# A three-layer transformer block on one core: when the last stage's base product is made, and which engine empties the FFN's sum banks

## The reference

```python
x = x + xattn0(layernorm(x), ctx)        # 32 query heads on 8 kv heads, RMS norms, Wo
x = x + ffn0(layernorm(x))               # 4-bit weights; silu(x Wg) * (x Wu), times Wd; 512 -> 1376 -> 512
x = x + xattn1(ctx, layernorm(x), ctx)   # softmax over tokens of ctx^T x, times ctx; no weights
x = x + ffn1(layernorm(x))
# ffn1:
base   = einsum('bsi,oi->bso', x, W_org)
q      = einsum('bi,ki->bk', x.mean(axis=1), Wq)
coeffs = softmax(einsum('bk,ek->be', q, lora_keys) / sqrt(128))
h      = einsum('bsi,eir->bser', x, lora_down)
delta  = einsum('be,bser,ero->bso', coeffs, h, lora_up)
return base + delta
```

## Time and profile before

| | us |
|---|---|
| median of 3 runs (lowest, highest) | 1201.81 (1201.21, 1204.52) |
| the profiled execution, its time | 1201.67 |
| its span | 1199.9 |
| TensorE busy in it | 1127.4 (94%) |
| VectorE, ScalarE, GpSimd busy | 755.0, 542.7, 416.3 |

### The profile page before, as it was taken

How to read it: one execution, slowest core, us unless ns; L and a number is a source line. 1 busy time by engine, 2 the same in 40 slices (tenths; PEclk the granted TensorE clock), 3 DMA queues, 4 the chain that set the end, 5 groups by cost and what they waited for, 6 DMA issues and landing times. The chain is left out here.

```text
span 1199.9 us, 19956 instructions
## 1 busy us (share of the span) xinstructions
PE 1127.4 (94%) x6643; PEld 963.4 (80%) x6643; DVE 755.0 (63%) x1572; ACT 542.7 (45%) x1437; POOL 416.3 (35%) x421
## 2 busy tenths in 40 slices
PE   4899999999999999999999988789999999898998
PEld 3799899898899898899899878567777777676776
DVE  7555555555555555555555777799954666687863
ACT  4444554544454544454544544343323445454541
POOL 4433332332322332323332433154422324554531
PEclk7999999999999999999999999999999999798999
DMA  6211111101011101011100010022202245133300
GB/s 210 76 36 33 26 33 32 36 23 35 24 35 32 34 25 35 23 36 32 33 19 11 22 46 1 18 80 80 75 25 54 62 106 124 43 74 77 88 1 36
DMA packets 48731, 56.65 MB, mean 47 GB/s; under 512 B 10822, under 2 KB 29270, under 8 KB 48620
## 3 DMA queue, kind: packets, MB, share of 16 engines
q1 hardware_dynamic: 48620, 55.26, 17.2%
HBM read 40.56 MB, written 2.10 MB: 36 GB/s over the span
## 5 line engine op out<-in xcount | busy, mean ns | idle before, releaser
L387 PE MATMUL bank<-wqkv,kvT 128*128 128x256 f32 x1536 | 201.2, 288 | 8.7 <-DVE vv L577 8.6
L387 PEld LDWEIGHTS bank<-wqkv,kvT 128*128 128x128 f32 x1536 | 189.3, 193 | 10.6 <-DVE vv L577 10.6
L432 PE MATMUL bank<-wo,aoT 128*128 128x512 f32 x768 | 192.0, 399 | 5.7 <-DVE acc L573 5.7
L375 PE MATMUL bank<-wqkv,kvT 128*128 128x512 f32 x768 | 189.2, 396 | 5.6 <-issue 4.0
L375 PEld LDWEIGHTS bank<-wqkv,kvT 128*128 128x128 f32 x768 | 141.7, 191 | 33.2 <-issue 6.2
L432 PEld LDWEIGHTS bank<-wo,aoT 128*128 128x128 f32 x768 | 139.5, 188 | 33.3 <-DVE aoT L568 6.3
L673 POOL TENSOR_TENSOR rms<-msq,half_neg 128x4 f32<-128x4 f32 x64 | 64.4, 1007 | 226.0 <-DVE msq L584 225.8
L560 ACT ACTIVATE prob<-bank,nmax 128x128 f32<-128x128 f32 x256 | 90.3, 372 | 2.1 <-DVE nmax L597 2.1
L538 ACT ACTIVATE qsq<-bank 128x512 f32<-128x512 f32 x64 | 38.2, 597 | 117.0 <-PE bank L375 117.0
L1916 POOL TENSOR_TENSOR pr<-pr,rc 128x512 f32<-128x512 f32 x64 | 66.6, 1044 | 70.7 <-DVE rc L1785 70.6
L676 POOL TENSOR_TENSOR rms<-msq,half_neg 128x2 f32<-128x2 f32 x64 | 44.6, 696 | 134.1 <-DVE msq L593 134.1
(11 more groups left out here) (176 smaller groups left out, 2210.3 us busy)
## 6 DMA issues: line engine op xcount, KB each, us to landing
wqkv_raw<-in_L_xattn_Wq_dram SPq DMA_DIRECT2D x32, 256.0 KB, 2.5
wo_raw<-in_L_xattn_Wo_dram SPq DMA_DIRECT2D x32, 256.0 KB, 2.7
qS<-qhl SPq DMA_DIRECT2D x32, 256.0 KB, 3.8
kS<-chl SPq DMA_DIRECT2D x32, 128.0 KB, 3.0
packed<-_L_ffn_gate_qweight_dram SPq DMA_DIRECT2D x40, 64.0 KB, 2.3
packed<-in_L_ffn_up_qweight_dram SPq DMA_DIRECT2D x40, 64.0 KB, 2.3
packed<-_L_ffn_down_qweight_dram SPq DMA_DIRECT2D x10, 256.0 KB
acc<-in_x_dram SPq DMA_DIRECT2D x8, 256.0 KB, 5.6
```

Of the source, the lines that this page charges most:

```text
L375: mm = pe.matmul(b_q[:, :], kvT[:, l, kt, p, 1:3, :], wqkv[:, par, r, kt, 0:QW], start=(kt == 0 and n == 0), stop=(kt == KT - 1 and n == 2))
L387: mm = pe.matmul(b_kv[:, b * 256:(b + 1) * 256], kvT[:, l, kt, p, 2 * b:2 * b + 2, :], wqkv[:, par, r, kt, QW:QKV], start=(kt == 0 and n = ...
L432: mm = pe.matmul(b_o[:, :], aoT[:, l, h, :, :], wo[:, par, r, h, :], start=(h == 0 and n == 0), stop=(h == G - 1 and n == 2))
```

## The change

The base product of pairs 0 to 5 gets its own sum: it ends its accumulation, VectorE adds it to `acc` (`add_base`), and the delta starts a fresh sum later. That lets base pieces stand anywhere, and the table puts them in slots 25 to 28, 37, 38, 41, 42, 53, 54, 57 and 58. Deltas of pairs 0 to 3 follow their ranks at once. The ffn0 sums of pairs 5 to 7 are copied out of PSUM by ScalarE in slot 25 (`act_down`) and added to `acc` by GpSimd in slots 27, 29 and 31. The two-bank scheme begins at slot 26. The copies and low parts of `up` move from slots 25 to 28 to slots 26, 28, 30 and 32.

```diff
-        WIDE = 30
+        WIDE = 26
+        m_b = [bank[5]] * 6 + [bank[3], bank[7]]
         def t_bank(t):
-            return bank[3] if t < WIDE else bank[(3, 7)[t % 2]]
+            return bank[3] if t < WIDE - LT else bank[(3, 7)[t % 2]]
...
+        for c, at_base in ((0, (25, 27)), (1, (37, 41)), (2, (53, 57))):
...
+            if c < 2:
+                LATE.update({(16 * c + 33 + 2 * i + r, 0): ("delta", 2 * c + i, r) for i in range(2) for r in range(2)})
...
         def pe_base(pe, p, r):
...
-                if p < HP and p % 2 == 0:
-                    pe.wait_ge(s_hv4, KT * (p // 2 + 1))
-                elif p < HP:
+                if p == 0:
+                    pe.wait_ge(s_yd, 1)
+                elif p < 6 and p % 2 == 0:
                     pe.wait_ge(s_y4, p)
-                elif p < HP + 2:
-                    pe.wait_ge(s_e1, TILES + p - HP - 1)
+                elif p < 6:
+                    pe.wait_ge(s_yb, p)
...
+            if p < 6 and r == 1:
+                mm.then_inc(s_ob, 1)
...
         def pe_delta(pe, p, r):
...
+                if p < HP and p % 2 == 1:
+                    pe.wait_ge(s_y4, p)
+                elif HP <= p < HP + 2:
+                    pe.wait_ge(s_e1, TILES + p - HP - 1)
...
-                                   start=False, stop=(t == KT - 1 and k == 2))
+                                   start=(p < 6 and t == 0 and k == 0), stop=(t == KT - 1 and k == 2))
...
         def act_slot(act, k):
+            if k == FFN_END + 1:
+                act_down(act, 0)
             # exp of tile k stands here
+            if k == FFN_END + 1:
+                act_down(act, 1)
+                act_down(act, 2)
+        def act_down(act, n):
+            if n == 0:
+                act.wait_ge(s_d, 2 * FT)
+            act.activation(dsum[:, n, :], f_d[n + 1][:, :], ACT.Copy).then_inc(s_yd, 1)
...
         def dve_slot(dve, k):
+            if k in BASE_DONE:
+                add_base(dve, BASE_DONE[k])
             if k in DELTA_DONE:
                 add_out(dve, DELTA_DONE[k])
...
-            if FFN_END < k <= FFN_END + HP:
-                add_down_one(dve, HP + k - FFN_END - 1)
+            if k == FFN_END + 1:
+                add_down_one(dve, HP)
...
+        def add_base(dve, p):
+            dve.wait_ge(s_ob, p + 1)
+            dve.tensor_tensor(acc[:, p, :], m_b[p][:, :], acc[:, p, :], ALU.add).then_inc(s_yb, 1)
...
         def pool_slot(pool, k):
+            if k in (27, 29, 31):
+                n = (k - 27) // 2
+                pool.wait_ge(s_yd, n + 1)
+                pool.tensor_tensor(acc[:, HP + 1 + n, :], acc[:, HP + 1 + n, :], dsum[:, n, :], ALU.add).then_inc(s_yp, 1)
```

More of the change, by code:

```diff
@@ L239, in block_kernel @@
         cT = at(227488, "cT", [P, KT, B], F32)
-        cexp = at(214048, "cexp", [B, EXP, RANK], F32)
+        dsum = at(214048, "dsum", [P, 3, D], F32)
+        cexp = at(220192, "cexp", [B, EXP, RANK], F32)
         s_const = sem("s_const")
@@ L1202, in block_kernel @@
             sem(f"s_{n}") for n in ("h4", "hv4", "hh4", "hl4", "o4", "y4", "cv", "ce"))
+        s_yd, s_yp, s_ob, s_yb = sem("s_yd"), sem("s_yp"), sem("s_ob"), sem("s_yb")
         CW = 256
@@ L1324, in dve_stats @@
         def dve_stats(dve, q):
-            dve.wait_ge(s_y2, q + 1)
+            if q <= HP:
+                dve.wait_ge(s_y2, q + 1)
+            else:
+                dve.wait_ge(s_yp, q - HP)
             dve.bn_stats(st3[:, :], acc[:, q, :]).then_inc(s_bn3, 1)
@@ L1439, in pe_weights @@
                 pe.wait_ge(s_n1, KT * (n + 1))
-            if t > WIDE + 1:
+            if t > WIDE - LT:
                 pe.wait_ge(s_p1l, t - 1)
-            elif t == WIDE + 1:
-                pe.wait_ge(s_y2, PAIRS)
+            elif t == WIDE - LT:
+                pe.wait_ge(s_yd, 3)
             elif t >= 1:
@@ L1461, in pe_values @@
             elif m == 0 and n == 6:
-                pe.wait_ge(s_y2, PAIRS)
+                pe.wait_ge(s_y2, HP + 1)
             elif m == 0:
@@ L1471, in block_kernel @@
         LATE = {}
[L1472 to L1481, removed]
+        for c, at_base in ((0, (25, 27)), (1, (37, 41)), (2, (53, 57))):
+            for i in range(2):
+                LATE.update({(at_base[i] + r, 0): ("base", 2 * c + i, r) for r in range(2)})
+            LATE.update({(16 * c + 29 + j, 0): ("rank", 4 * c + j) for j in range(KT)})
+            if c < 2:
+                LATE.update({(16 * c + 33 + 2 * i + r, 0): ("delta", 2 * c + i, r) for i in range(2) for r in range(2)})
+        LATE.update({(66, 0): ("delta", 4, 0), (67, 0): ("delta", 4, 1),
                      (69, 0): ("delta", 5, 0), (69, 1): ("delta", 5, 1), (70, 0): ("base", 6, 0)})
+        BASE_DONE = {k + 1: piece[1] for (k, h), piece in LATE.items() if piece[0] == "base" and piece[2] == 1}
         RANK_DONE = {k + 1: (piece[1],) for (k, h), piece in LATE.items() if piece[0] == "rank"}
@@ L1539, in pe_base @@
                 for k, (lp, rp) in enumerate(PASSES):
-                    pe.matmul(m_o[p][:, :], x4_tile(lp, p)[:, kt, :], woT[:, rp, kt, :],
-                              start=(kt == 0 and k == 0), stop=False)
+                    mm = pe.matmul(m_b[p][:, :], x4_tile(lp, p)[:, kt, :], woT[:, rp, kt, :],
+                                   start=(kt == 0 and k == 0), stop=(p < 6 and kt == KT - 1 and k == 2))
+            if p < 6 and r == 1:
+                mm.then_inc(s_ob, 1)
         def pe_rank(pe, n):
@@ L1547, in pe_rank @@
             pe.wait_ge(s_x4l, 2 * (c + 1))
[L1548 to L1551, removed]
+            if n < 3 * KT and j == 0:
+                pe.wait_ge(s_yb, 2 * c + 2)
             elif n <= 3 * KT:
@@ L1584, in pe_extra @@
                 pe.wait_ge(s_p1l, k - LT + 1)
-            elif k == context_slot(4):
-                pe.wait_ge(s_y2, PAIRS)
+            elif k == WIDE:
+                pe.wait_ge(s_yd, 2)
             else:
@@ L1689, in act_slot @@
                 act.activation(dn[:, HI, t, :], draw[:, t, :], ACT.Copy).then_inc(s_dnh, 1)
-            if 25 <= k <= 28:
-                t = k - 25
+            if k in (26, 28, 30, 32):
+                t = (k - 26) // 2
                 act.wait_ge(s_ld_u, 16)
@@ L1886, in rank_times @@
                               ALU.mult).then_inc(s_hv4, 1)
+        def add_base(dve, p):
+            dve.wait_ge(s_ob, p + 1)
+            dve.tensor_tensor(acc[:, p, :], m_b[p][:, :], acc[:, p, :], ALU.add).then_inc(s_yb, 1)
         def add_out(dve, p):
             dve.wait_ge(s_o4, p + 1)
+            if p < 6:
+                dve.wait_ge(s_yb, p + 1)
             dve.tensor_tensor(acc[:, p, :], m_o[p][:, :], acc[:, p, :], ALU.add).then_inc(s_y4, 1)
```

4 lines of the change are left out of this document (2 added, 2 removed).

## The result

The changed kernel is slower: 1212.08 us (median of 4 runs, 1210.10 to 1213.05) against 1201.51 us, a ratio of 1.0083 with a 95% interval of 1.0067 to 1.0100. I had forecast 1200.1, with a range up to 1205.3. The profiled execution took 1213.05 us, its span is 1211.2.

A forecast was written before the change was run, and what follows sets the result against it. TensorE, busy 94% of the span, was taken as the bound. The terms summed to -2.8 us, -1.7 with 1.1 for the clock: 1201.81 - 1.7 = 1200.1 us; own range 1198 to 1202.5, 8 in 10 between 1194.8 and 1205.3.

The forecast's parts named there:

- A: Slots 25 to 29: four base pieces fill TensorE's waits, but GpSimd is late with `pr` 27; -1.6 us.
- B: Slots 33 to 37: the first delta loses its cover and waits 3.0 us for GpSimd's `hs`; +3.1 us.
- C: Slots 37 to 44: moved base pieces end VectorE's waits for TensorE, extra adds cost some back; -0.3 us.
- D: Slots 49 to 53: as B without the extra GpSimd work, delta waits 2.1 us; +1.9 us.
- clock in B and D: After the waits in B and D the clock may fall; +1.1 us, from a range of 0 to 6.
- E: Slots 53 to 61: as C without an attention layer norm; 0.9 won at slot 58, 1.2 at 61; -1.2 us.
- F: Slots 65 to 70: four base pieces leave, 5.6 us of work, 0.9 goes to a new wait; -4.7 us.
- The lower clock, slower: Rival, chance 0.16: half clock at the deltas of slots 33 to 36 and 49 to 52 costs matmul time; 1206.6 us.
- Its sign: Half clock for over 10 us in slots 33 to 52 was to show the forecast wrong.
- The early fillers bring nothing: Rival, chance 0.08: A is -0.4 or worse, every base waiting for the previous one's add in bank 5; 1201.3 us.
- All three rivals: Delta waits cost nothing (chance 0.26, 1194.0 us); lower clock, slower (0.16); early fillers bring nothing (0.08).
- that rule: Port sharing: GpSimd's three `acc` adds could each hold up an `xn` once, up to 0.9 us worse in slots 26 to 34.

The follow-up runs named there:

- experiment 11: Changed kernel, order kept, but the values products of tiles 20 to 23 go to bank 4 instead of bank 1; 1209.31 us.
- experiment 1: Changed kernel, but in slot 26 the values product stands behind the base piece and the mean query again; 1205.83 us.
- experiment 3: Changed kernel with the base pieces of slots 41 and 57 (pairs 3 and 5) one slot later; 1209.52 us.
- experiment 2: Changed kernel with the deltas of pairs 0 to 3 one slot later, bases of slots 37 and 53 moved to 38 and 54; 1205.18 us.
- experiment 5: Changed kernel with the edits of experiment 1, experiment 2 and experiment 3 together; 1197.39 us.
- experiment 8: Kernel before the change, with only the base pieces of pairs 4 and 5 moved to slots 57 to 60, own sum in bank 5; 1199.02 us.
- experiment 6: Kernel of experiment 5 with GpSimd's three adds in slots 31, 38 and 46 instead of 27, 29 and 31; 1195.63 us.
- experiment 9: Kernel of experiment 5 with the ffn0 sums of pairs 5 to 7 added by VectorE in slot 25 again; ratio 0.9955 to before.
- 10: Kernel of experiment 6 with GpSimd's second and third adds one slot later (39 and 47); ratio 0.9967 to before.

## Why the prediction was wrong, step by step

The terms as measured, in the profiled execution of after against that of before:

| term | predicted | measured | |
|---|---|---|---|
| A, slots 25 to 30 | -1.6 | +4.3 | the failed step |
| B, 33 to 37 | +3.1 | +4.3 | right, the clock's price included |
| C, 37 to 45, and 45 to 49 | -0.3 | +2.3, -0.7 | missed a wait and a fall of the clock |
| D, 49 to 53 | +1.9 | +2.0 | right |
| clock in B and D | +1.1 | in B | |
| E, 53 to 61 | -1.2 | +1.7 | missed the same wait |
| F, 64 to 68 | -4.7 | -4.7 | right |

The rest, slots 30 to 33, 61 to 64 and the end, is -0.4; the sum from slot 25 is +8.8, and 2.5 of the span's 11.3 stood there at slot 25 already.

**Term A failed, and at one step.** I added up "0.54 values" for slot 26, the price of the product, and asked only the banks of the scores and the piece whether they were free. The front of the document shows that the product moves ahead of the piece, and I used that order for the spacing of starts. I didn't ask what the product waits for, though in slot 26 it opens a new sum in the one bank that all values shared until then. Experiment 11 shows in its trace that this bank is the cause of the wait, experiment 1 in trace and timed runs what the order with it costs. The price was 2.73 us of waiting and, behind it, near 7 us at half clock; slots 25 to 30 took 4.3 us more than before instead of 1.6 less. What I did expect there, GpSimd late with `pr` 27 and a wait of 2.4, didn't show, because TensorE was later still; once the bank wait is gone, it appears at 1.87 us (experiment 11) or 0.82 (experiment 1). GpSimd's add, which I took at 1.04, takes 1.26 to 1.30. With the product behind the piece (experiment 1) the term is -0.5, at the poor end of my bounds. My bounds of -3.5 to -0.4 were bounds on the mechanisms I had listed.

**Terms C and E failed too, and in part in one way.** I won 0.9 and more "at slot 58" by filling empty slots, without looking up when the piece's input is made. The x4 low part of pairs 3 and 5 is made by VectorE in slots 41 and 57 themselves. In E experiment 3 gives back 1.6 us of the 2.9 that I was off. The other 1.3 isn't explained: even then slots 53 to 61 take as long as before, and my gains of 0.9 and 1.2 don't show. In C the larger part is the clock, which fell in slot 40: experiment 1, with the same table and the same wait but no fall there, takes 24.92, which is +0.3 against before and not +2.3.

**Terms B and D were right in mechanism and size**: waits of 2.83 and 2.11 where I had 3.0 and 2.1, and 1.16 for VectorE's add. B, D and the clock's price were 6.1 together, and 6.3 were measured. I had put the clock at 1.1; the piece of slot 33 held the next scores for 2.64 us instead of 1.40, that is 1.2 more, and slots 49 to 53 stayed at the upper clock. Experiments 2 and 5 show that the whole of both goes with one slot's delay, so the cover itself was not needed.

**Term F was right**, in size and in place. It is the largest single gain of the change: experiment 8 has it alone, with its price in slots 57 to 60, and is 2.9 us faster than before. All the rest, with its waits mended, adds 1.6 us in experiment 5 and 3.4 in experiment 6.

**The rivals.** "The lower clock, slower" came nearest with 1206.6, but not by its mechanism: mean clock from slot 25 is 0.94 after and 0.93 before, and the loss is 8.8 us of idle time. Its sign did come, half clock for over 10 us in slots 33 to 52 (about 13.6 us), but 6.8 us of that stood there before, and none of it fell in slots 49 to 52, where it should have. "The early fillers bring nothing" had the right place, A at -0.4 or worse, but the wrong bank, 5 instead of 1, and 1201.3. All three rivals and my forecast shared the missing wait, and so the range ended at 1205.3.

## What to carry to other kernels

When an order changes, write down for each instruction that moves forward what it waits for, the product that opens a new sum above all, and not only for the new pieces: its price is the wait of the engine plus all that is queued behind it. A filler belongs one slot after its input is made, not in the slot where the gap is: here that slot cost 1.2 to 1.6 us of waiting each time. And look first at the work that can leave a stretch in which the busiest engine has no pauses: here the four pieces that left the end won 4.7 us there and cost 2.9 to 3.6 where they went.

## What the hardware showed that I had not expected

**A GpSimd operation can hold up a tiny VectorE operation, to its very end.** The coefficients' scaling (`lg`, 4x8) takes 0.22 us in the trace of before. In experiment 1 it stands beside GpSimd's add:

```profile
1045.39 1.34 DVE L1894 TENSOR_SCALAR lg<-cf,cstat 4x8 f32<-4x8 f32 x1
```

```profile
1045.45 1.26 POOL L1967 TENSOR_TENSOR acc<-acc,dsum 128x512 f32<-128x512 f32 x1
```

It ends at 1046.73, the add at 1046.71. It had started while GpSimd's `pr` still ran (until 1045.49), and the add went ahead of it. In experiment 6 it stands beside `pr` instead and takes 0.73, ending 0.02 behind that as well (1043.84, 1043.82). In after it is the copy behind it, `cexp`, that takes 1.44 instead of 0.42:

```profile
1051.63 1.44 DVE L1896 COPY cexp<-lg 4x512 f32<-4x512 f32 x1
```

The Trainium skill (SBUF — State Buffer, Who interferes with whom) says that VectorE in its two-port mode and GpSimd take turns, an instruction at a time, on one pair of ports; these rows agree. It can also go the other way: in experiment 1 an `xn` that starts at 1112.01 takes its 0.54, and GpSimd's `hs` low part, from 1112.09, takes 1.05 instead of 0.74. I had weighed that rule on the layer norm's `xn` alone, and the copy that TensorE waits for (1.79) was in the same queue.

**Half clock came with a wait in one execution and not with the same wait in another.** After the 2.73 us of slot 26 it held from about 1038.0 to 1044.8, and the pieces took up to 2.37 us; in the earlier trace rows 1.93 us of waiting stood ahead of it, and in experiment 9 it began during the wait of 2.10. But the 2.11 us of slot 49 in after left the clock up (its piece takes 1.63). With the wait of 1.9 us in slot 45 it came in experiments 6 and 10 and not in 5 and 9, and with the 1.59 us ahead of the early base pieces it came twice in experiment 2 and not in experiment 1. In experiment 11, 1.87 us of waiting in slot 29 left the clock at 1.00:

```profile
1042.40 0.66 PE L1457 MATMUL bank<-ident,pr 128*128 128x128 f32 x4 [1.87 <-POOL pr L1943]
1042.81 0.70 PE L1473 MATMUL bank<-pmT,vS 128*128 128x512 f32 x2
1043.36 1.57 PE L1567 MATMUL bank<-x4a,dn 128*128 128x256 f32 x12
```

The earlier trace rows has a fall without any long wait, and in slot 40 of after one came where experiment 1, with the same table, has none. The Trainium skill (TensorE: Matmul & The Clock Gate, HAM oscillation) ties a fall to long pauses; the trace doesn't agree that only those do it. What decides it in each case isn't settled. What the runs do show is its weight: in experiment 5, where no wait of TensorE is over 1.9 us, the clock is up from slot 25 to the last us, and 7.0 of the 7.3 us gained over before are booked there.
